# VectorE adds up the four corners of a sampled tile before TensorE turns it

## The reference

```
offset = conv3x3(x)                        # 18 channels: 9 taps x (dy, dx)
py, px = row - 1 + ky + dy, column - 1 + kx + dx
y0, x0 = floor(py), floor(px);  ty, tx = py - y0, px - x0
sampled = gather(y0, x0) * (1-ty)*(1-tx) + gather(y0, x0+1) * (1-ty)*tx
        + gather(y0+1, x0) * ty*(1-tx)   + gather(y0+1, x0+1) * ty*tx
out = einsum('bckhw,ock->bohw', sampled, weight)       # 9 taps k, 128 x 128 each
```

## Time and profile before

| what | value |
|---|---|
| median of 3 runs | 1898.65 us |
| the runs | 1882.53, 1898.65, 1901.92 us |
| span of the profiled execution | 1901.1 us; the nearest run is 1901.92 |
| TensorE matmul, weight load, busy | 1391.0 us (73%), 963.0 us (51%) |
| VectorE busy | 1142.3 us (60%) |
| ScalarE busy | 431.3 us (23%) |
| GpSimd busy | 1006.9 us (53%) |
| granted TensorE clock, mean | 0.852 |

### The profile page before, as it was taken

How to read it: one execution, slowest core, us unless ns; L and a number is a source line. 1 busy time by engine, 2 the same in 40 slices (tenths; PEclk the granted TensorE clock), 3 DMA queues, 4 the chain that set the end, 5 groups by cost and what they waited for, 6 DMA issues and landing times.

```text
span 1901.1 us, 22950 instructions
## 1 busy us (share of the span) xinstructions
PE 1391.0 (73%) x7851; PEld 963.0 (51%) x7894; DVE 1142.3 (60%) x1483; ACT 431.3 (23%) x1390; POOL 1006.9 (53%) x977
## 2 busy tenths in 40 slices
PE   5899897999999778755568765764766657656566
PEld 2455553544444334324556655554665546656566
DVE  5478687899999999766563723333614532544332
ACT  1330001233443225224532111111112111111112
POOL 6078585344434323555455665555565555666661
PEclk9899998999999979887679777787877877787778
DMA  4140000111111105444467655666566656565651
GB/s 157 34 145 2 1 0 13 27 51 51 51 51 51 34 17 149 125 145 145 119 184 236 183 173 166 203 185 177 175 173 182 198 157 192 167 206 164 185 161 63
DMA packets 111113, 232.85 MB, mean 122 GB/s; under 512 B 14676, under 2 KB 60500, under 8 KB 110748
## 3 DMA queue, kind: packets, MB, share of 16 engines
q0 software_dynamic: 58176, 191.30, 34.5%
q1 hardware_dynamic: 52828, 40.17, 6.7%
HBM read 205.15 MB, written 26.26 MB: 122 GB/s over the span
## 4 chain that ended last, share of the span: by engine, by line
PE 44%; another core or an unknown queue 15%; issue 15%; DVE 6%; ACT 4%; POOL 0%; DVEq 0%; ACTq 0%; POOLq 0%
PE score L1450 16%; PE turn_ps L1459 8%; PE score L1426 3%; PE score L1428 3%; PE score L1427 3%; DVE max_region L1850 2%; PE lead_score L1360 2%; PE lead_score L1428 2%; PE lead_score L1427 2%; PE lead_score L1426 2%; PE turn_ps L1330 1%; PE lead_score L1389 1%; DVE x L254 1%; ACT max_region L1631 1%
## 5 line engine op out<-in xcount | busy, mean ns | idle before, releaser
L2037 POOL DMA_INDIRECT code_region<-corners,lead_region x252 | 240.8, 956 | 164.9 <-PE score L1450 69.7
L1850 DVE SCALAR_TENSOR_TENSOR max_region<-score,nc,max_region 128x512 f32<-128x512 f32 x324 | 230.2, 739 | 34.9 <-PE score L1428 26.8
L742 POOL TENSOR_TENSOR prod_acc<-prod_acc,prod_pool 128x752 f32<-128x752 f32 (+8 forms) x112 | 151.8, 1355 | 97.5 <-DVE prod_pool L715 90.0
L1459 PE MATMUL turn_ps<-code_region,max_region 128*128 128x128 f32 x864 | 136.5, 312 | 74.3 <-issue 39.0
L1725 DVE TENSOR_TENSOR lead_region<-lead_score,lead_region 128x54 f32<-128x54 f32 x24 | 5.1, 213 | 296.7 <-PE lead_score L1389 200.1
L1459 PE MATMUL turn_ps<-max_region 128*128 128x128 f32 x432 | 91.5, 369 | 124.2 <-ACT max_region L1631 85.3
L1450 PE MATMUL score<-ident,code_region 128*128 128x128 f32 x1008 | 149.9, 310 | 39.6 <-issue 39.6
L2037 POOL DMA_INDIRECT late_region<-corners,lead_region x126 | 119.2, 946 | 94.6 <-PE score L1450 46.9
L2037 POOL DMA_INDIRECT early_region<-corners,lead_region x136 | 128.7, 946 | 76.7 <-issue 43.0
L1459 PEld LDWEIGHTS turn_ps<-code_region,max_region 128*128 128x128 f32 x864 | 123.2, 221 | 83.5 <-issue 57.5
L2037 POOL DMA_INDIRECT max_region<-corners,lead_region x130 | 123.7, 951 | 75.6 <-issue 36.2
(11 more groups left out here) (273 smaller groups left out, 2932.4 us busy)
## 6 DMA issues: line engine op xcount, KB each, us to landing
corners<-lead_region SPq DMA_DIRECT2D x72, 192.0 KB
corners<-lead_region SPq DMA_DIRECT2D x8, 576.0 KB
code_rows<-codes_n SPq DMA_DIRECT2D x8, 516.0 KB, 4.3
codes_t<-in_codes_t SPq DMA_DIRECT2D x8, 512.0 KB, 3.8
codes_n<-in_codes SPq DMA_DIRECT2D x8, 512.0 KB, 4.5
code_region<-corners,lead_region POOLq DMA_INDIRECT x252
x<-in_x SPq DMA_DIRECT2D x2, 1152.0 KB, 6.7
out<-x SPq DMA_DIRECT2D x4, 576.0 KB
```

Of the source, the lines that this page charges most:

```text
L742: pool.tensor_tensor(to, to, v, ALU.add).then_inc(pooled, 1)
L1459: mm = pe.matmul(yps, w_tap[j // B][:, 3 * g + k, :], turned_x[g][:, k * P:(k + 1) * P], start=g + k == 0, stop=g + k == 4)
L1850: dve.scalar_tensor_tensor(r, score[SLOT[k]], nc2[:, m:m + 1], r, ALU.add, ALU.max).then_inc(dve_took, 1)
L2037: pool.indirect_dma_start(quad(T, k), None, table[j].rearrange("n s c -> n (s c)"), bass.IndirectOffsetOnAxis(index[j % B][:, at:at + 1], 0))\
```

## The change

From tile 5 on (`SUMMED` = 5) VectorE does two instructions for a tile: the same multiply, and then one reduction that adds up the four corners of each tap and channel. Its input is read with the corner as the innermost index, so that each element lies 128 elements (512 bytes) from the last; it writes 9 x 128 = 1152 elements to one of two buffers. These lie in the weights of the depthwise layer (`wk`) and between two regions, for which the slot in `late_region` begins 1044 elements later. Before it writes, it waits until TensorE has turned tile T-2. TensorE turns nine blocks instead of 36 from that buffer, without accumulating. GpSimd's gather of tile T, from tile 10 on, waits for VectorE's sum of tile T-5 instead of TensorE's turn.

```
         SLOTS = len(quads)
+        SUMMED = max(BY_SCALAR) + 1
+        summed_quads = [depthwise.wk.rearrange("p t o -> p (t o)"), region_sums[:, 0:TAPS * P]]
...
                     for k in range(3):
-                        for c in range(CORNERS):
-                            mm = pe.matmul(tps[g][:, k * P:(k + 1) * P],
-                                           quad(T, 3 * g + k)[:, c * P:(c + 1) * P], ident,
-                                           start=c == 0, stop=c == CORNERS - 1, is_transpose=True)
+                        at = (3 * g + k) * P
+                        rows = [summed_quads[T % 2][:, at:at + P]] if T >= SUMMED else [
+                            quad(T, 3 * g + k)[:, c * P:(c + 1) * P] for c in range(CORNERS)]
+                        for c, v in enumerate(rows):
+                            mm = pe.matmul(tps[g][:, k * P:(k + 1) * P], v, ident,
+                                           start=c == 0, stop=c == len(rows) - 1, is_transpose=True)
...
-                dve.tensor_tensor(q4, bc(wps[:, u * n:(u + 1) * n], P), q4, ALU.mult).then_inc(weighted, 1)
+                product = dve.tensor_tensor(q4, bc(wps[:, u * n:(u + 1) * n], P), q4, ALU.mult)
+                if T < SUMMED:
+                    product.then_inc(weighted, 1)
+                    return
+                chain(product)
+                if T >= SUMMED + 2:
+                    dve.wait_ge(turn_done, 3 * TPC + 3 * (T - 2) + 3)
+                dve.tensor_reduce(summed_quads[T % 2].rearrange("p (k c) -> p k c", c=P),
+                                  quads[slot(T)].rearrange("p k (j c) -> p k c j", c=P), AX, ALU.add)\
+                    .then_inc(weighted, 1)
...
-                if T > SLOTS:
+                if T >= SUMMED + SLOTS:
+                    apart.wait_ge(weighted, by_dve(T - SLOTS) + 1)
+                elif T > SLOTS:
                     apart.wait_ge(turn_done, 3 * TPC + 3 * (T - SLOTS if T > SLOTS + 2 else T - SLOTS - 1) + 3)
...
-        max_region = tools.sb(ctx, "max_region", [P, 10240])
-        late_region = tools.sb(ctx, "late_region", [P, 5652])
+        last_region = tools.sb(ctx, "last_region", [P, 10240 + 5652])
+        max_region, late_region = last_region[:, 0:10240], last_region[:, 10240:]
+        sums_region = last_region[:, 10240 - 512:10240 + 1044]
```

More of the change, by code:

```diff
@@ L1082, in finale @@
     L0 = EARLY + 1
-    region_code, region_lead, region_early, region_max, region_late = places
+    region_code, region_lead, region_early, region_max, region_late, region_sums = places
     ch, cl = code_views(region_code)
@@ L1130, in finale @@
         quads = [r[:, at:at + gathered].rearrange("p (k q) -> p k q", k=TAPS) for r, at in (
-            (region_early, 0), (region_code, 0), (region_code, gathered), (region_max, 0), (region_late, 0))]
+            (region_early, 0), (region_code, 0), (region_code, gathered), (region_max, 0), (region_late, 1044))]
         SLOTS = len(quads)
+        SUMMED = max(BY_SCALAR) + 1
+        summed_quads = [depthwise.wk.rearrange("p t o -> p (t o)"), region_sums[:, 0:TAPS * P]]
         early_quads = (xt[:, 0:4 * QUAD], region_early[:, gathered:gathered + QUAD], y1_quads)
@@ L2135, in program @@
         early_region = tools.sb(ctx, "early_region", [P, 5120])
-        max_region = tools.sb(ctx, "max_region", [P, 10240])
-        late_region = tools.sb(ctx, "late_region", [P, 5652])
+        last_region = tools.sb(ctx, "last_region", [P, 10240 + 5652])
+        max_region, late_region = last_region[:, 0:10240], last_region[:, 10240:]
+        sums_region = last_region[:, 10240 - 512:10240 + 1044]
         finale(nc, tools, a, code_rows, x, xpad, ident, gm32, gm8, nc2, depthwise, between,
-               (code_region[:], lead_region[:], early_region[:], max_region[:], late_region[:]), out)
+               (code_region[:], lead_region[:], early_region[:], max_region, late_region, sums_region), out)
 def layouts(i):
```

## The result

The changed kernel takes 1929.95 us (median), the kernel before 1898.15; the ratio is 1.0155, 95% interval 1.0104 to 1.0205. It is 1 to 2% slower, where 1810 and faster was forecast. It lies inside the stated range (1725 to 1970) only because that range was drawn to hold the rivals with a dear sum; that is no support for the forecast. The profiled execution has a span of 1928.3 us, 27.2 more than before.

What follows compares the result with a forecast made beforehand. It took a loop of waits as the bound, no engine full, TensorE pacing GpSimd's gathers. From the nearest run's 1901.9 us, 76 (period) and 14 (tail) off give 1812, on the median's scale 1810; range 1725 to 1970.

Steps and rivals of the forecast that it cites:

- (a): TensorE, 36 corner turns to nine: a quick tile goes from 7.2 to 4.3 us, a slow one from 33.6 to 22.6.
- (b): VectorE's added sum costs 4.95 us, bounds 6.3 and 8.1; VectorE needs 10.7 us a tile, hidden below GpSimd's 11.25.
- (c): Slots freed by VectorE's sum: GpSimd runs some four tiles on before TensorE's lag stops it, instead of at nearly every tile.
- (d): Balance of GpSimd and TensorE from tile 10 to 71: period falls from 14.30 to 13.05 us, gain 76 us.
- (e): Tail from the last multiply's start to the span's end: 24.6 us instead of 38.5, 14 us less.
- Hops at the dear row: Rival, chance 0.14: VectorE's sum costs 1.73 ns an element, 8.1 us, VectorE 14.0 us a tile; 1870 us in all.
- hops slow the sum past the period: Rival, chance 0.24: VectorE becomes the bound, sum 9.8 us, 15.6 us a tile, 1970 us; break-even 8.75 us a sum.
- TensorE still paces: Rival, chance 0.13: nearly all TensorE taps fall into the slow back-to-back state, period some 14.0 us; 1867 us in all.

Runs made afterwards that it cites:

- e3_nine: The kernel before with TensorE turning only the first corner of each tap from tile 5 on, nine blocks and no sum: 1867.14 us, 0.976.
- e1_near: The changed kernel with the sum reading four adjacent elements instead of the four corners, so no read hops (other numbers): 1983.32 us, 1.033 of the kernel before.
- e9_pause: The changed kernel, its sum untouched, plus two idle GpSimd multiplications before each tile's gathers from tile 10 on: 1905.31 us, 0.9995 of the kernel before.
- e7_near_pause: The changed kernel with the sum over adjacent elements, plus two idle GpSimd multiplications before each tile's gathers from tile 10: 1846.79 us, 0.964 of the kernel before.

## Why the prediction was wrong

Four runs make a table, as ratios to the kernel before:

| sum | gathers unpaused | 2.57 us pause a tile |
|---|---|---|
| 8.0 us (hops) | 1.0155 (the change) | 0.9995 |
| 4.95 us | 1.033 | 0.964 |

The forecast was 0.953. With the forecast's sum and paused gathers 0.964 was measured, with the dear sum besides 0.9995, and with the pause taken away 1.0155. Three more views bear on single steps: the last tile's turns in the changed kernel; TensorE's busy time and clock with no gather left (columns as above), before and in the changed kernel; and ScalarE's copies of the next tile right behind the late result of the earlier trace rows.

```profile
1911.23 2.18 PE L1455 MATMUL score<-ident,last_region 128*128 128x128 f32 x9 [7.81 <-DVE last_region L1896]
```
```profile
1870.00:1890.00 20.00, 19.42 (x177) 19.23 (x175) 0.81 (x2) 5.47 (x14) 0.00 (x0) 1.00 0.00 1
```
```profile
1900.00:1918.00 18.00, 8.85 (x48) 8.47 (x46) 14.39 (x10) 2.88 (x7) 0.00 (x0) 0.65 0.00 0
```
```profile
1271.46 0.87 ACT L1631 COPY code_region<-score 128x384 f32<-128x384 f32 x2
```

- **(a) failed in its prices.** Nine quick turns were to take 1.0 us; with no gather left they take 2.18, 0.24 us each instead of 0.109. Before, TensorE was busy 19.4 of 20 us there, at a granted clock of 1.00 (2.4 GHz); now it stands idle 8 us ahead of each of the last tiles, and 0.65 is granted, a mean of both levels (1.2 and 2.4 GHz). From the last sum to the last result it is 5.5 us, not 3.0. And the 16.3 us of the earlier trace rows are not the price of 18 taps: two groups of the next tile were ready with that result, so 24 of its turns fall into them too (as in eight of the eleven waits of 14 to 16 us for a result), and the slow tile of 33.6 us counts part of the turns twice. That fewer turns free TensorE held in part: 2.4% with everything else as before (e3_nine).
- **(b) failed.** The sum was taken at 4.95 us because a single stepping source of two had cost nothing in the earlier trace rows; it costs 8.0, 1.70 ns an element with the 0.15 us taken off. The bound of 8.1 from the earlier trace rows came near, though the instruction behind it steps in its output as well. The Trainium skill's figure for one source that hops at every element (page "Vector Engine (DVE) Microarchitecture Reference", section "Measured stream behaviour on trn2", 1.73 ns, there for hops of 4 KiB) agrees with the trace; its remark on a stream that alternates between two regions at the full rate, which the prediction set against it, didn't carry over to four corners. That the hops make the price is shown by e1_near. It is worth 3.5% where GpSimd is paced (0.9995 against 0.964). That this one number decides most was wrong too: at 4.95 us, without a pause, the kernel is slower still.
- **(c) and (d) failed**, and by more. They took GpSimd's stops for a cost that would become rarer, and TensorE beside gathers for merely slow (22.6 us a tile). Where gathers run on over several tiles, a result can stay out until about when they pause: 38 and 42 us in the change. With the very sum that was forecast, the period was 15.1 us, not 13.05 (e1_near). That the clock fell to 0.67 is not the cause: in e9_pause, at 0.68 in the same stretch, no such wait is left. In the change itself, with VectorE as the bound, this costs only the two waits before sums, 14.3 + 16.4 = 31 us, which e9_pause gives back.
- **(e) failed** with (b): four tiles stand before VectorE at the end, and the tail grew by 29 us. Where GpSimd is the bound, the step was right: in e7_near_pause the span ends 40.1 us after the last tile's first gather, 11.8 us less than before; 14 were forecast, and most of the rest is the last tile's turns and taps at their slower price (4.9 us from the last sum to the last result, not 3.0).
- **The rivals.** *Hops at the dear row* had the sum's price right, and nearly VectorE's time for a tile (its own terms make 13.85, not 14.0; measured 13.75), but the time (1870) wrong: it put the period against the gathers', but a chain that is bound by VectorE begins at tile 5 with the gathers four tiles ahead, so its time is 962 + 67 x 13.75 + 16.5 = 1900. With the 31 us of waits that is 1931; the profiled span is 1928.3. For the same reason the break-even of *hops slow the sum past the period*, 8.75 us a sum, was too high: at 8.0 us the kernel already loses, and even with the pause it only breaks even. That rival's 1970 came from a price of 9.8 us that was not met. *TensorE still paces* named the place of the second loss, and made it far too small.

Why the gathers hold TensorE up is not settled. The runs show that the bytes are not the cause, and that a pause of one piece lifts it; what TensorE and the gathers share, why tile 33's result came quickly in the midst of a run, and whether GpSimd's work or the number of rows counts, was not tried, and neither was a kernel that adds up all four corners cheaply without stopping GpSimd and has a pause.

## What to carry to other kernels

A wait that seems only to cost may be what another engine lives on: before taking one away, look at what the engine behind it does when it runs unchecked, and try the relieved engine with an idle pause in its place. Price a strided read by the dearest row of its engine that steps at all, as long as no row hops like it, and price a chain that becomes the bound from where it begins, with what already stands before it, not by the rate of the engine that feeds it. Here a sum over a far index was cheaper as additions over contiguous runs (3.9 us against 8.0), and what the second SBUF source does to GpSimd belongs in the price.

## What the hardware showed that was not expected

- TensorE's results can stay out for 38 to 42 us while GpSimd issues indirect transfers 1.25 us apart, at 173 GB/s as at 57. TensorE's own rows, whose ends are modelled, have tile 34's taps end at 1380.4; the result was copied at 1414.9.
- One pause of 2.57 us in 13.6 us all but removes this (longest wait 8.2 us); one of 1.67 us, or three of 0.7, do so only in part (12.2 and 21.3 us).
- An addition of two SBUF sources on VectorE lengthens a gather's issue from 0.94 to 3.06 us; the multiply with weights in PSUM, and reductions, leave it at 0.95.
